# Local attention on one core: Newton's steps for the inverse norms moved from VectorE to GpSimd, their first guess made one stretch sooner

## What is computed

```python
q, k, v = split(shift_token(x) @ wqkv, 3)        # 8 heads of 64
q = q / clip(norm(q), 1e-12) * qs                # norm over the 64 of a head
k = k / clip(norm(k), 1e-12) * ksc
q = q * cos * scale + rotate_half(q) * sin * scale
k = k * cos / scale + rotate_half(k) * sin / scale
sim = einsum(q * 8, k)    # each block of 64 queries sees its own block and the one before
attn = softmax(where(mask, -max, sim))
x = x + einsum(attn, v) @ wo
```

## Time and profile before

| | |
|---|---|
| time, median of 3 runs (lowest to highest) | 2676.96 us (2676.78 to 2678.5) |
| time of the profiled execution | 2674.28 us |
| its span in the profile | 2672.5 us |
| busy share of the span: PE, DVE, ACT, POOL | 90%, 78%, 54%, 44% |
| local attention of layer 0, from first projection to last sum | about 774 to 987 us |
| local attention of layer 1 | about 1045 to 1258 us |

### The profile page before, as it was taken

How to read it: one execution, slowest core, us unless ns; L and a number is a source line. 1 busy time by engine, 2 the same in 40 slices (tenths; PEclk the granted TensorE clock), 3 DMA queues, 4 the chain that set the end, 5 groups by cost and what they waited for, 6 DMA issues and landing times.

```text
span 2672.5 us, 41317 instructions
## 1 busy us (share of the span) xinstructions
PE 2413.3 (90%) x14910; PEld 1127.4 (42%) x14910; DVE 2081.4 (78%) x3341; ACT 1452.3 (54%) x2541; POOL 1173.9 (44%) x980
## 2 busy tenths in 40 slices
PE   6799985988868977887699999999999999999897
PEld 5444434453335654565433333433343334333344
DVE  7798876428879965996588899888889988889642
ACT  5576652627647753675365555455545554555462
POOL 2211110306835531553056666566656665566630
PEclk9899988999989999999899999999999999999999
DMA  5000001010000000000100000000000000000000
GB/s 211 1 1 1 1 1 56 1 44 1 32 16 1 2 32 1 1 1 17 44 1 9 9 9 5 9 9 10 9 9 6 9 9 9 10 9 9 5 1 16
DMA packets 21128, 42.00 MB, mean 16 GB/s; under 512 B 10494, under 2 KB 12670, under 8 KB 19772
## 3 DMA queue, kind: packets, MB, share of 16 engines
q1 hardware_dynamic: 20924, 39.35, 4.3%
HBM read 34.90 MB, written 4.45 MB: 15 GB/s over the span
## 4 chain that ended last, share of the span: by engine, by line
PE 66%; DVE 23%; issue 6%; ACT 3%; POOL 1%; DMA 0%; DVEq 0%; POOLq 0%; ACTq 0%; SPq 0%
PE PS L2672 16%; PE PS L2663 15%; PE PS L1236 6%; PE PS L2635 5%; DVE WK L2188 2%; DVE NR L274 2%; DVE NR L2876 2%; PE PS L1218 2%; DVE WK L2164 2%; PE PS L680 2%; PE PS L682 2%; PE PS L681 2%; DVE WK L271 1%; DVE WK L2171 1%; PE PS L2618 1%
## 5 line engine op out<-in xcount | busy, mean ns | idle before, releaser
L2778 ACT ACTIVATE WK<-PS 128x1024 f32<-128x1024 f32 x512 | 497.6, 1022 | 458.1 <-PE PS L2663 452.4
L2955 POOL TENSOR_TENSOR W<-W,WK 128x512 f32<-128x512 f32 x448 | 575.8, 1287 | 383.4 <-DVE W L2894 382.1
L2876 DVE TENSOR_REDUCE NR<-PS 128x2 f32<-128x1024 f32 x512 | 625.3, 1223 | 131.7 <-PE PS L2636 115.9
L2672 PE MATMUL PS<-WK,W 128*64 128x512 f32 x2048 | 494.1, 603 | 0.0
L2663 PE MATMUL PS<-WK 64*128 64x512 f16 (+1 forms) x4096 | 484.0, 376 | 0.6 <-issue 0.6
L2894 DVE TENSOR_TENSOR W<-W,WK 128x512 f32<-128x512 f32 x448 | 342.8, 767 | 9.9 <-ACT WK L2778 9.4
L2663 PEld LDWEIGHTS PS<-WK 64*128 64x128 f16 (+1 forms) x4096 | 199.2, 94 | 219.8 <-ACT WK L2778 6.5
L2672 PEld LDWEIGHTS PS<-WK,W 128*64 128x64 f32 x2048 | 124.1, 136 | 246.9 <-issue 168.9
L2635 PE MATMUL PS<-WK 64*128 64x512 f16 x512 | 195.4, 382 | 5.5 <-DVE NR L2876 4.9
L2636 PE MATMUL PS<-WK 64*128 64x512 f16 x512 | 195.4, 382 | 0.0
L2203 POOL TENSOR_TENSOR WK<-WK,W 128x512 f32<-128x512 f32 x64 | 113.3, 1792 | 176.1 <-DVE WK L2148 93.8
(11 more groups left out here) (371 smaller groups left out, 4326.7 us busy)
## 6 DMA issues: line engine op xcount, KB each, us to landing
XB<-l_rdens SPq DMA_DIRECT2D x62, 128.0 KB, 2.9
W<-in_mw SPq DMA_DIRECT2D x8, 512.0 KB, 11.8
W<-in_l2w SPq DMA_DIRECT2D x1, 3114.0 KB, 12.0
W<-in_f1w SPq DMA_DIRECT2D x1, 2816.0 KB, 18.6
W<-in_l3w SPq DMA_DIRECT2D x1, 2816.0 KB, 9.9
W<-in_f3w SPq DMA_DIRECT2D x1, 2816.0 KB, 9.8
W<-in_mw SPq DMA_DIRECT2D x8, 256.0 KB, 12.3
la_second_tables<-W SPq DMA_DIRECT2D x1, 2048.0 KB, 6.3
```

Of the source, the lines that this page charges most:

```text
L2672: m = e.matmul(k.PS[64 * i:64 * i + 64, 4, :], self.V[:, kt, g, :], self.PTB[kt // 2 % 2][:, kt % 2, i, :], start=kt == 0, stop=kt == NT - 1)
L2778: e.activation(self.PTB[kt // 2 % 2][:, kt % 2, :, :], self.k.PS[:, 2 * (kt % 2):2 * (kt % 2) + 2, :], ACT.Exp, scale=1.0 / 64).then_inc(s ...
L2876: e.tensor_reduce(self.PM[ji % 2][:, u // 4, :, u % 4], self.k.PS[:, bk:bk + 2, :], AX.X, ALU.max).then_inc(self.maxes.sem)
L2955: e.tensor_tensor(ac, ac, p, ALU.add).then_inc(self.acc1.sem)
```

## The change

1. `rsqrt` is split: `rsqrt_guess` (two instructions) and `rsqrt_newton` (nine). The layer norms still call both in turn. The local attention calls the guess on VectorE, and a new `pool_newton` on GpSimd, where a Newton step is four instructions of 128x16 instead of three: 12 dependent instructions a strip, counted by a new semaphore `newton`.
2. On VectorE the squares' sum and the guess of strip i (not i-1) stand after the scaling of strip i-1 and before the second maximum of strip i-2. Strip 0's are made in turn 0 of the loop.
3. On GpSimd the 12 instructions stand after the sine products of strip i-1 and before the probabilities of strip i-3. The scaling L2155 waits for them.
4. On ScalarE the squares stand right behind the projection's copy, and no more between the exponentials.

```diff
--- before.py
+++ after.py
@@ -261,22 +261,47 @@
             e.tensor_copy(k.XT[0:64, b * 512:(b + 1) * 512], k.bank(b % 2, p1=64)).then_inc(self.lower.sem)
 
 
-def rsqrt(k, e, o, v, n, slot, step, at):
-
-
-    a, b = k.NR[:, 0, slot:slot + n], k.NR[:, 1, slot:slot + n]
+def rsqrt_guess(k, e, o, v, n, slot, step, at):
+
+
+    a = k.NR[:, 0, slot:slot + n]
     e.wait_ge(*step(at))
     e.tensor_single_scalar(a.bitcast(I32), v.bitcast(I32), 1, ALU.logical_shift_right).then_inc(step.sem)
     e.wait_ge(*step(at + 1))
     e.tensor_scalar(o.bitcast(I32), a.bitcast(I32), -1.0, 1597463007.0, ALU.mult, ALU.add).then_inc(step.sem)
+    return at + 2
+
+
+def rsqrt_newton(k, e, o, v, n, slot, step, at):
+
+    a, b = k.NR[:, 0, slot:slot + n], k.NR[:, 1, slot:slot + n]
     for r in range(3):
+        e.wait_ge(*step(at + 3 * r))
+        e.tensor_tensor(a, o, o, ALU.mult).then_inc(step.sem)
+        e.wait_ge(*step(at + 1 + 3 * r))
+        e.scalar_tensor_tensor(out=b, in0=a, scalar=-0.5, in1=v, op0=ALU.mult, op1=ALU.mult).then_inc(step.sem)
         e.wait_ge(*step(at + 2 + 3 * r))
+        e.scalar_tensor_tensor(out=o, in0=b, scalar=1.5, in1=o, op0=ALU.add, op1=ALU.mult).then_inc(step.sem)
+    return at + 9
+
+
+def pool_newton(k, e, o, v, n, slot, step, at):
+
+    a, b = k.NR[:, 0, slot:slot + n], k.NR[:, 1, slot:slot + n]
+    for r in range(3):
+        e.wait_ge(*step(at + 4 * r))
         e.tensor_tensor(a, o, o, ALU.mult).then_inc(step.sem)
-        e.wait_ge(*step(at + 3 + 3 * r))
-        e.scalar_tensor_tensor(out=b, in0=a, scalar=-0.5, in1=v, op0=ALU.mult, op1=ALU.mult).then_inc(step.sem)
-        e.wait_ge(*step(at + 4 + 3 * r))
-        e.scalar_tensor_tensor(out=o, in0=b, scalar=1.5, in1=o, op0=ALU.add, op1=ALU.mult).then_inc(step.sem)
-    return at + 11
+        e.wait_ge(*step(at + 1 + 4 * r))
+        e.tensor_tensor(b, a, v, ALU.mult).then_inc(step.sem)
+        e.wait_ge(*step(at + 2 + 4 * r))
+        e.tensor_scalar(a, b, -0.5, 1.5, ALU.mult, ALU.add).then_inc(step.sem)
+        e.wait_ge(*step(at + 3 + 4 * r))
+        e.tensor_tensor(o, o, a, ALU.mult).then_inc(step.sem)
+
+
+def rsqrt(k, e, o, v, n, slot, step, at):
+
+    return rsqrt_newton(k, e, o, v, n, slot, step, rsqrt_guess(k, e, o, v, n, slot, step, at))
 
 
 class LayerNorm:
@@ -1843,7 +1868,7 @@
 
 
 
-    STEPS = 13
+    STEPS, NEWTON = 4, 12
 
     def __init__(self, k, ld, l, tables, before=None):
         self.k, self.ld, self.l, self.begin, self.before = k, ld, l, Barrier(k), before
@@ -1879,6 +1904,7 @@
         self.v = k.counter("la_v", 16)
         self.sq = k.counter("la_squares", 16)
         self.step = k.counter("la_norm_steps", 16 * self.STEPS)
+        self.newton = k.counter("la_newton_steps", 16 * self.NEWTON)
         self.sin = k.counter("la_sines", 32)
         self.cos = k.counter("la_cosines", 16)
         self.rotsum = k.counter("la_rotated", 16)
@@ -2040,6 +2066,7 @@
         for i in range(NT + 4):
             if i < NT:
                 self.act_project(e, i)
+                self.act_squares(e, i)
             if 4 <= i:
                 self.act_turn_probs(e, i - 4, 0)
             if i < NT:
@@ -2050,8 +2077,6 @@
                 self.act_exp(e, i - 2, 0)
             if 4 <= i:
                 self.act_weigh(e, i)
-            if i < NT:
-                self.act_squares(e, i)
             if 2 <= i < NT + 2:
                 self.act_exp(e, i - 2, 1)
             if 1 <= i <= NT:
@@ -2130,7 +2155,6 @@
         for i in range(NT + 5):
             if 1 <= i <= NT:
                 self.dve_cosines(e, i - 1)
-                self.dve_squares(e, i - 1)
             if 5 <= i:
                 t = i - 5
                 e.wait_ge(*self.out(t + 1))
@@ -2139,8 +2163,6 @@
                 den = self.DEN[(i - 3) % 2]
                 e.wait_ge(*self.exp(2 * (i - 3) + 2))
                 e.reciprocal(den[:, 1, :], den[:, 0, :]).then_inc(self.rden.sem)
-            if 1 <= i <= NT:
-                self.dve_norms(e, i - 1)
             if 1 <= i <= NT:
                 ro = self.RO[(i - 1) % 2]
                 e.wait_ge(*self.sin(2 * i))
@@ -2151,8 +2173,11 @@
             if 1 <= i <= NT:
                 r4 = ro.rearrange("p (h d) -> p h d", h=16)
                 e.wait_ge(*self.rotsum(i))
-                e.wait_ge(*self.step(self.STEPS * i))
+                e.wait_ge(*self.newton(self.NEWTON * i))
                 e.tensor_tensor(r4, r4, self.RS.unsqueeze(2).broadcast_to([P, 16, 64]), ALU.mult).then_inc(self.rot.sem)
+            if i < NT:
+                self.dve_squares(e, i)
+                self.dve_norms(e, i)
             if 2 <= i < NT + 2:
                 self.dve_top(e, i - 2, 1)
 
@@ -2167,17 +2192,18 @@
 
         e.wait_ge(*self.sq(t + 1))
         if t:
-            e.wait_ge(*self.step(self.STEPS * t))
+            e.wait_ge(*self.newton(self.NEWTON * t))
         e.tensor_reduce(self.SS, self.SQ.rearrange("p (h d) -> p h d", h=16), AX.X, ALU.add).then_inc(self.step.sem)
 
     def dve_norms(self, e, t):
+
 
         k, step, at = self.k, self.step, self.STEPS * t
         if t:
             e.wait_ge(*self.rot(t))
         e.wait_ge(*step(at + 1))
         e.tensor_scalar(self.SS, self.SS, 1e-24, None, ALU.max).then_inc(step.sem)
-        rsqrt(k, e, self.RS, self.SS, 16, 32, step, at + 2)
+        rsqrt_guess(k, e, self.RS, self.SS, 16, 32, step, at + 2)
 
     def dve_top(self, e, t, hg):
         lo = 0 if t else 64
@@ -2202,6 +2228,8 @@
                 for hf in range(2):
                     e.tensor_tensor(p5[:, :, :, hf, :], q5[:, :, :, 1 - hf, :],
                                     self.SN[:, t, :, hf * 32:hf * 32 + 32].unsqueeze(2).broadcast_to([P, 2, 8, 32]), ALU.mult).then_inc(self.sin.sem)
+                e.wait_ge(*self.step(self.STEPS * i))
+                pool_newton(k, e, self.RS, self.SS, 16, 32, self.newton, self.NEWTON * t)
             if 3 <= i:
                 t = i - 3
                 px, den, lo = self.PX[t % 2], self.DEN[t % 2], 0 if t else 64
```

## The result

| | before | after |
|---|---|---|
| median (lowest to highest) | 2677.08 us (2676.78 to 2678.5) | 2696.13 us (2694.55 to 2697.61) |
| profiled execution, its span | 2674.28, 2672.5 us | 2697.61, 2695.8 us |
| ratio | 1 | 1.007, 95% interval 1.0053 to 1.0087 |
| period in the middle of a stage | 11.98 us | 12.49 us |

What follows compares the result with a forecast made beforehand. VectorE was taken to bound the 11.98 us period; afterwards GpSimd's chain makes it 12.65. Per stage 1.9 + 2.0 + 8.0 = 11.9, two stages 23.8, on 2674.3 gives 2698.1, plus 2.7: 2701 us, range 2662 to 2725.

Steps and rivals of the forecast that it cites:

- Bound of the kernel before: VectorE, without idle gaps, sets the middle-of-stage period of 11.98 us, part of its time being waiting for GpSimd.
- the interlock: Certain VectorE instructions never run inside a GpSimd instruction; one engine waits, about 1.2 us a period in the old Newton chain.
- TensorE's floor of 10.90: The shortest period TensorE allows: 11.98 us less its single wait of 1.08 for the scaling.
- Price of Newton on GpSimd: 12 dependent 128x16 instructions: 9 x 0.30 + 3 x 0.33 = 3.7 us, bounds 3.5 and 4.9.
- The period: Time per strip in the middle of a stage after the change: 12.65 us, 0.67 more than 11.98.
- T = m + 7.35: One period laid out: T the period, m the guess's end at 5.2 to 5.35, giving 12.55 to 12.7 us.
- S's ring: TensorE, first maximum, scaling, sum, guess, second maximum, exponentials, back to TensorE; 11.15 us in the forecast without holds.
- The holds: VectorE's waits for GpSimd in the layout: scaling 0.3 us, guess behind the second sine product until 4.78.
- The chain named as the bound: GpSimd's Newton, probabilities and sine products, with VectorE's long instructions between: 12.0 us plus what the guess adds.
- rival A: GpSimd's short instructions do not contend with VectorE's: period 11.15 us, 2659 us, not slower; chance 0.16.
- rival B: Newton on GpSimd takes 3.0 us, 0.25 apart; GpSimd's chain 12.0 long, about 2680 us; chance 0.12.
- The start of a stage: Newton has no cover at strip 0: +1.9 us; longer periods until strip 3: +2.0 in all.

Runs made afterwards that it cites:

- e8: Kernel before, with GpSimd's two multiplications by the inverse sums touching 4 columns of 192 instead of all: 2644.07 us.
- e7: Kernel before, with two Newton steps instead of three on VectorE: 2657.42 us, period 11.36.
- e5: Changed kernel with Newton back on VectorE, guess and Newton a stretch sooner, behind the second maximum: 2642.18 us.
- e9: Changed kernel with GpSimd's sine products also waiting for the scaling of the strip before: 2696.53 us, period 12.47.
- e2: Changed kernel with one Newton step instead of three on GpSimd: 2680.55 us, period 12.08.
- e12: Changed kernel with two Newton steps on GpSimd and the sine products in four instructions of 128x256 instead of two: 2665.19 us.
- e6: Changed kernel with two Newton steps instead of three on GpSimd: 2691.5 us, period 12.54.
- e4: Changed kernel with the second maximum right behind the scaling, ahead of the squares' sum and guess: 2679.41 us, period 11.85.
- e3: Changed kernel with six Newton steps instead of three on GpSimd: 2787.83 us, period 15.4.
- e1: Changed kernel's order, with Newton's nine instructions back on VectorE, behind the guess and ahead of the second maximum: 2745.6 us.

## Why the prediction was right, and where it wasn't

**Bound of the kernel before, and the interlock:** right; e8 and e7 came within 1 us of what was expected of them, and TensorE's floor of 10.90 is the 10.84 of e5.

**Price of Newton on GpSimd:** 3.7 us forecast, 0.30 and 0.33 apart; measured 0.30 apart, some 3.5 in all, and 5.39 with two VectorE instructions in it (5.6 forecast). The Trainium skill ("GPSIMD Engine Reference", Engine selection) has elementwise work with two inputs about 2 times slower on GpSimd. The rows don't agree for 16 elements: 0.30 against 0.21 us from start to start, 1.4 times; at twice 0.21, Newton would have taken 5.0 us.

**The period:** 12.65 forecast, 12.49 measured, and from a layout with a wrong share for each part. The layout, T = m + 7.35, went along S's ring: 11.15 and two holds. The ring is 11.4: TensorE's stretch from turning the probabilities to the first maximum took 4.74 us and not 4.62, and the guess starts 1.31 us behind the start of the sum (900.63, 901.94), where 1.13 was the step to L2137, which doesn't need the sum. The holds were put at 0.3 for the scaling and 1.2 for the guess; the scaling had 1.1 and the guess none. So the sum is close in part by luck: 0.25 too little in the ring and 0.4 too much in the holds. One hold of about 1.1 comes out whoever is held (e9: 12.47 against 12.49), but not in every phase: 0.66 in e2, nothing in e12.

**The chain named as the bound:** wrong. The text said that GpSimd's chain, 12.0 plus the guess, made the period; e6 left it 1.2 us shorter and the period stayed. GpSimd's sum is the bound only with the second maximum first and three steps (e4) or with a longer Newton (e3). The prediction had seen the real one, "the second maximum no longer follows the scaling at once", but counted it as TensorE's waiting, not as the cause. It priced the ring only in rival A, without holds, and no rival had the ring with a hold in it. That 12.0 and the ring with its holds lay so near each other is luck too. For the same reason rival B (cheap Newton, no change in time) was priced wrongly: a third less Newton gained 5 us of the 19, most of it in a stage's first strips, and two thirds less 16.

**The start of a stage:** 1.9 forecast for strip 0, 1.5 measured. The layout itself had Newton's end at 787.0, 9.8 us behind the copy, and the scaling came at 9.76; the 0.3 added for "somewhat later" didn't come. For strips 1 to 3 it was 2.0 against 1.1. **The 12 periods behind it:** 8.0 forecast, 6.7 measured in layer 0 and 6.2 in layer 1. **Behind strip 15,** where the forecast had nothing: 1.1 in layer 0 and 0.6 in layer 1. In layer 0 TensorE stood idle for 1.8 of 4 us there and then ran at a granted clock of 0.68 (989 to 993 us), where before it had 1.00. Over both stages the forecast's 23.8 becomes 5.4 + 13.0 + 1.7 = 20 us.

**Signs that were named:** steps 0.3 apart with two of 1.2 (seen), TensorE waiting for L2124 (0.85 us, and still 0.4 for the scaling), GpSimd idle 0.5 us (0.78), VectorE idle for 2 us (4.0).

## What to carry to other kernels

Idle time on another engine isn't yet room for work when the two engines' instructions exclude each other: lay out one period, and mark for each instruction whether the interlock holds it and who is queued behind it. The same move of Newton to GpSimd gained 49 us in the change's order (e1 to after) and cost 37 in the other (e5 to e4). Here the whole gain lay in the order: make the squares' sum, guess and Newton a period early but *behind* the second maximum, and the kernel before becomes 34 us faster with no work moved. And the length of the single instruction can matter more than the sum: with each of GpSimd's two sine products cut in halves the kernel was 26 us faster (e6 to e12), though the four together take longer.

## What was not expected of the hardware

- When GpSimd has its next instruction ready, a waiting one of VectorE's still goes first at the border between two: L271, after 1.15 us, in the earlier trace rows; the scaling after 0.17 us in e12 (900.08, border at 900.25). One that comes with the border, to within 0.03 us, waits for the whole next one, and it costs 1.1 us (e6).
- A GpSimd instruction held by VectorE counts as busy, like VectorE's: the 128x16 steps show 1.1 to 1.26 us for 0.22, so the busy time of each engine contains its waiting for the other.
- TensorE's waits of 2.3 to 2.7 us a period were followed, in some periods, by a stretch at half clock (granted 0.57 in 4 us), and those periods were 0.9 to 1.5 us longer (e1; in e3 every second period from 894 us on has a granted clock of 0.89); with waits of 0.85 it stayed at 1.00 in three periods of after. Why one period and not the next isn't shown.
